# Transformer block on one core: the start-up steps of the attention stage in another order, and the gates computed by GpSimd from copies that ScalarE makes

## Reference

```python
mod = (silu(c) @ wmod).reshape(2, 6, 1, 512)
sa, ca, ga, sb, cb, gb = (mod[:, i] for i in range(6))
ga = (2 * (ga >= 0) - 1) * maximum(abs(ga), 0.25)
gb = (2 * (gb >= 0) - 1) * maximum(abs(gb), 0.25)
h = layernorm(x) * (1 + ca) + sa
x = x + ga * attention(h, Wq, Wk, Wv, Wo)      # rotary positions, causal softmax, grouped heads
h = layernorm(x) * (1 + cb) + sb
x = x + gb * ffn(h)                            # ternary weights, silu(gate) * up, rms norm
```

## Time and profile before

| | |
|---|---|
| median of 3 runs | 1857.39 us (1854.3 to 1860.57) |
| the profiled execution, its own time | 1858.29 us |
| its span in the trace | 1856.3 us |
| granted TensorE clock, mean | 0.987 |
| PE busy | 1747.3 us (94%) |
| DVE / ACT / POOL busy | 1259.0 / 1147.6 / 964.8 us |

### The profile page before, as it was taken

The page is one execution under the profiler, slowest core; times in us unless marked ns, Lnnn a source line. Parts: engine busy times, 40 slices in busy tenths (PEclk is TensorE's granted clock), DMA queues, the critical chain, the costliest instruction groups (busy, mean ns, idle before and its releaser), DMA issues. The chain is left out here.

```text
span 1856.3 us, 28089 instructions
## 1 busy us (share of the span) xinstructions
PE 1747.3 (94%) x9505; PEld 1394.7 (75%) x9505; DVE 1259.0 (68%) x2078; ACT 1147.6 (62%) x2315; POOL 964.8 (52%) x773
## 2 busy tenths in 40 slices
PE   6899999999999999999999999996999999999998
PEld 3577787777777777778777777774788778888886
DVE  5787887788788778788778878884333355545343
ACT  4578787777777777877777777784322354323322
POOL 1256667666667666666766666753000035444454
PEclk9999999999999999999999999998999999999999
DMA  6433444344344344344434434425655400101000
GB/s 229 121 94 103 120 102 124 100 109 121 88 131 114 86 123 112 92 117 108 121 103 108 125 83 134 119 82 163 208 179 177 134 29 1 52 1 51 1 29 23
DMA packets 174969, 190.95 MB, mean 103 GB/s; under 512 B 31456, under 2 KB 117736, under 8 KB 174832
## 3 DMA queue, kind: packets, MB, share of 16 engines
q1 hardware_dynamic: 137840, 140.99, 26.7%
q10 hardware_dynamic: 36992, 48.25, 9.4%
HBM read 86.12 MB, written 31.74 MB: 63 GB/s over the span
## 5 line engine op out<-in xcount | busy, mean ns | idle before, releaser
L926 DVE TENSOR_TENSOR p_lo<-ps_b,p_hi 128x512 fp32r<-128x512 f32 x576 | 395.3, 686 | 194.7 <-ACT p_hi L829 190.8
L844 ACT ACTIVATE p<-ps_b,negm 128x640 f32<-128x640 f32 (+7 forms) x512 | 381.9, 749 | 111.4 <-DVE negm L934 108.5
L829 ACT CAST p_hi<-ps_b 128x512 fp32r<-128x512 f32 x576 | 337.0, 588 | 156.9 <-PE ps_b L748 154.2
L934 DVE TENSOR_REDUCE negm<-ps_b 128x1 f32<-128x640 f32 (+7 forms) x512 | 375.8, 744 | 34.1 <-PE ps_b L738 33.4
L748 PE MATMUL ps_b<-ident,p 128*128 128x128 f32 x2304 | 350.3, 275 | 3.1 <-DVE p_lo L926 2.1
L736 PE MATMUL ps_b<-k_hh,q_hl 128*128 128x512 f32 (+3 forms) x768 | 270.1, 352 | 37.0 <-ACT p L844 36.0
L762 PE MATMUL ps_b<-p_hi,v_hl 128*128 128x512 f32 x576 | 276.9, 481 | 16.4 <-ACT o_sb L837 16.1
L748 PEld LDWEIGHTS ps_b<-ident,p 128*128 128x128 f32 x2304 | 259.0, 141 | 37.3 <-DVE p_lo L926 5.1
L737 PE MATMUL ps_b<-k_l,q_hl 128*128 128x512 f32 (+3 forms) x768 | 256.1, 346 | 0.0
L763 PE MATMUL ps_b<-p_lo,v_hl 128*128 128x512 f32 x576 | 227.6, 395 | 0.0
L736 PEld LDWEIGHTS ps_b<-k_hh,q_hl 128*128 128x128 f32 x768 | 145.1, 189 | 87.4 <-ACT p L844 54.7
(11 more groups left out here) (156 smaller groups left out, 3202.6 us busy)
## 6 DMA issues: line engine op xcount, KB each, us to landing
rot_x<-rot_s SPq DMA_DIRECT2D x320, 64.0 KB, 2.0
q_hl<-rot_s SPq DMA_DIRECT2D x128, 128.0 KB, 2.5
q_hl<-rot_x SPq DMA_DIRECT2D x128, 128.0 KB, 2.5
rd_all<-reciprocals SPq DMA_DIRECT2D x128, 128.0 KB, 3.0
o_low<-o_sb ACTq DMA_DIRECT2D x128, 128.0 KB, 2.4
attention_out<-o_sb SPq DMA_DIRECT2D x128, 128.0 KB, 2.5
o_raw<-attention_out SPq DMA_DIRECT2D x32, 512.0 KB, 4.9
wf<-in_L_ffn_w_gate_up ACTq DMA_DIRECT2D x32, 256.0 KB, 3.0
```

What stands on the lines that cost most here:

```text
L829: act.copy(p_hi[:, T % P_RING, :], ps[:, T_BANK + T % 2, :]).then_inc(phi_ready, 1)
L844: act.activation(p_32[:, parity, h, column * P:column * P + nk], s, ACT.Exp, bias=negm[:, k:k + 1], scale=1.0, accum_out=den[:, parity, k: ...
L926: dve.tensor_tensor(p_lo[:, T % P_RING, :], ps[:, T_BANK + T % 2, :], p_hi[:, T % P_RING, :].bitcast(F32), ALU.subtract).then_inc(plo_read ...
L934: dve.tensor_reduce(negm[:, k:k + 1], s, AX.X, ALU.max, negate=True).then_inc(max_ready, 1)
```

## The change

The order of the start-up changes, and who makes the gates:
- Products 0 and 1 go to PSUM banks 2 and 3; product 0 no longer waits for ScalarE's reading of n = 1. Products 1, 2 and 3 are cut into halves of two pieces; gates' products are at T = 49/53 and 58/59 and no longer between the rows of scores. The turn of late shift and scale (`LATE_TURN`) goes from T = 70 to 62.
- The gates' part of `wmod` is loaded in the prologue, before the last 512 rows of x; for this the prologue's normalised rows go to `late.h32` and `late.xn`.
- ScalarE copies the gates out of PSUM at T = 61 (two copies of 2 x 512). GpSimd makes them in five operations of 2 x 1024, all at T = 66, ahead of what it has else in that step; VectorE has no part in it. The one fused VectorE operation at the end becomes two on GpSimd. The store goes from T = 71 to 70.
- Normalising of n = 2 goes from T = 44 to 41, its statistics from 36 to 37; writing of `h` for n = 3 from T = 59 to 62 to T = 56 to 59; `hT_lo` of n = 1 in part behind the first rotary, that of n = 2 in part ahead of the rotary of qx1.
- In the start-up, ScalarE's cast, GpSimd's low part and SP's place of qy0 and qy1 come twelve steps after the use's first instead of eight, eight and ten: T = 66 and 71.
- ScalarE runs a small exponential at T = 53 (`TABLE_AT`), and the casts of the constants go from T = 52 to 60.

```diff
-        xt, xn = [x_rows[:, n] for n in range(2)], [vectors.rows_at(n) for n in range(2)]
+        xt, xn = [x_rows[:, n] for n in range(2)], [late.h32, late.xn]
@@ prologue, sync
                 sp.dma_start(vectors.late[0][:, :, v, :], wm_v[:, :, place, :]).then_inc(vectors.late_in, 16)
+            vectors.load_gates(sp, wmod)
             load_x(3, late.xt[:, 1])
@@ step numbers
-LATE_AT, LATE_TURN, LATE_ROWS = (35, 41, 64, 66), 70, (45, 45)
-GATE_LOAD, GATE_STEPS, GATE_STORE = 50, 67, 71
-ROWS_STAT, ROWS_ROOT, ROWS_NORM, ROWS_TURN = (36, 49), (41, 50), (44, 54), (48, 58)
-ROWS_MOD = ((28, 29, 30, 31), (49, 50, 51, 51), (59, 60, 61, 62))
-ROWS_LOW = ((31, 32, 33, 34), (55, 55, 56, 56), (59, 60, 61, 62))
-CONSTS_AT, KEYS_AT, QUERY_SWAP = 52, 12, 59
+LATE_AT = ((35, 0, (0, 1, 2, 3)), (41, 1, (0, 1)), (43, 1, (2, 3)), (49, 2, (0, 1)), (53, 2, (2, 3)), (58, 3, (0, 1)), (59, 3, (2, 3)))
+LATE_BANK, LATE_ROWS, LATE_TURN = (2, 3, T_BANK, T_BANK + 1), (45, 45), 62
+GATE_STEPS, GATE_STORE = (61, 66, 66, 66, 66, 66), 70
+ROWS_STAT, ROWS_ROOT, ROWS_NORM, ROWS_TURN = (37, 49), (38, 50), (41, 54), (48, 58)
+ROWS_MOD = ((28, 29, 30, 31), (49, 50, 51, 51), (56, 57, 58, 59))
+ROWS_LOW = ((31, 32, 36, 36), (50, 51, 55, 55), (59, 60, 61, 62))
+CONSTS_AT, KEYS_AT, QUERIES_AT, QUERY_SWAP, TABLE_AT = 60, 12, 12, 59, 53
@@ tensor
-                    pe.wait_ge(late.h_ready, 2 * CT)
-                vectors.product(pe, ps[0:B, T_BANK + v % 2, :], vectors.late[v // 2], v % 2).then_inc(vectors.late_done, 1)
+                i = vectors.product(pe, ps[0:B, LATE_BANK[v], :], vectors.late[v // 2], v % 2, pieces)
+                if CT - 1 in pieces:
+                    i.then_inc(vectors.late_done, 1)
@@ scalar
+                if body.before(T, GATE_STEPS[0]):
+                    act.wait_ge(vectors.late_done, 4)
+                    for v in range(2):
+                        act.copy(o_sb[0:B, v, :], ps[0:B, LATE_BANK[2 + v], :]).then_inc(vectors.gate_copied, 1)
+                if body.before(T, TABLE_AT):
+                    act.activation(den[:, 1, :], ident[:, 0:len(ROWS)], ACT.Exp)
-                for g, n, _ in body.uses(T, 8, kinds=("qx", "qy")):
+                for g, n, _ in body.uses(T, 8, kinds=("qx",)) + body.uses(T, QUERIES_AT if body.g < 0 else 8, kinds=("qy",)):
@@ gates, off VectorE and onto GpSimd
-                    dve.tensor_copy(graw, ps[0:B, T_BANK:T_BANK + 2, :]).then_inc(vectors.gate_copied, 1)
-                    gate_chain.step(dve.tensor_scalar(gsgn, graw, 0.0, 2.0, ALU.is_ge, ALU.mult))
-                    gate_chain.step(dve.tensor_scalar(gsgn, gsgn, -1.0, None, ALU.add))
-                    gate_chain.step(dve.tensor_tensor(graw, graw, gsgn, ALU.mult))
-                    dve.scalar_tensor_tensor(out=graw, in0=graw, scalar=0.25, in1=gsgn, op0=ALU.max,
-                                             op1=ALU.mult).then_inc(vectors.gates_done, 1)
+                    pool.wait_ge(vectors.gate_copied, 2)
+                    gate_chain.step(pool.tensor_scalar(gsgn, graw, 0.0, 2.0, ALU.is_ge, ALU.mult))
+                    gate_chain.step(pool.tensor_scalar(gsgn, gsgn, -1.0, None, ALU.add))
+                    gate_chain.step(pool.tensor_tensor(graw, graw, gsgn, ALU.mult))
+                    gate_chain.step(pool.tensor_scalar(graw, graw, 0.25, None, ALU.max))
+                    pool.tensor_tensor(graw, graw, gsgn, ALU.mult).then_inc(vectors.gates_done, 1)
@@ gpsimd
             def step(body, T):
+                for n in range(1, 6):
+                    if body.before(T, GATE_STEPS[n]):
+                        gate_step(n)
-                for g, n, _ in body.uses(T, 8, kinds=("qx", "qy")):
+                for g, n, _ in body.uses(T, 8, kinds=("qx",)) + body.uses(T, QUERIES_AT if body.g < 0 else 8, kinds=("qy",)):
@@ sync
-                    for g, n, _ in body.uses(T, 10, kinds=("qx", "qy")):
+                    for g, n, _ in body.uses(T, 10, kinds=("qx",)):
                         place(g, n)
+                for g, n, _ in body.uses(T, QUERIES_AT if body.g < 0 else 10, kinds=("qy",)):
+                    place(g, n)
-                if body.before(T, GATE_LOAD):
-                    sp.wait_ge(vectors.late_done, 2)
-                    vectors.load_gates(sp, wmod)
```

More of the change, by code:

```diff
@@ L101, in __init__ @@
         self.late = [flat[:, at:at + size].rearrange("p (k v e) -> p k v e", k=CT, v=2) for at in (0, 2 * GQ * 9 * P - size)]
-        self.flat = flat
         self.late_in, self.gate_in = sem("late_in"), sem("gate_in")
@@ L106, in __init__ @@
         self.gate_copied, self.gate_link, self.gates_done, self.gates_out = [sem(n) for n in ("gcopied", "glink", "gates", "gout")]
-    def rows_at(self, n):
-        size = 4 * E
-        return self.flat[:, (2 + n) * size:(3 + n) * size].rearrange("p (t e) -> p t e", t=4)
     def load_gates(self, sp, wmod):
@@ L114, in load_gates, with product @@
             sp.dma_start(self.late[1][:, :, v, :], mod_columns(wmod)[:, :, GATE[v], :]).then_inc(self.gate_in, 16)
-    def product(self, pe, out, wm, v):
-        for kc in range(CT):
+    def product(self, pe, out, wm, v, pieces=range(CT)):
+        for kc in pieces:
             i = pe.matmul(out, self.cs[:].rearrange("p (b k) -> p k b", b=B)[:, kc, :], wm[:, kc, v, :],
@@ L153, in place @@
         self.xn = sb("xn_l", [P, 2 * P_RING, 512])[:, 0:4, :]
-        self.h32 = [sb("h32_l%d" % n, [P, 2, 512]) for n in range(2)]
+        self.h32 = sb("h32_l", [P, CT, 512])
     def statistics(self, dve, n, xt):
@@ L587, in late_h32 @@
         def late_h32(n, k):
-            return spare[:, k // 2, k % 2, :] if n == 1 else late.h32[k // 2][:, k % 2, :]
+            return spare[:, k // 2, k % 2, :] if n == 1 else late.h32[:, k, :]
         @block.sync
@@ L742, in turn @@
                 if g == 0 and T == 0:
-                    pe.wait_ge(vectors.gate_copied, 1)
+                    pe.wait_ge(vectors.gate_copied, 2)
                 if j == 0:
@@ L769, in late_turns, with late_product @@
                         pe.wait_ge(late.h_ready, 2 * CT + (k + 1 if n == 3 else 0))
+                    if k == 0 and n == 2:
+                        pe.wait_ge(vectors.late_rows, 2)
                     late.turn(pe, n, k, ps[:, turned_bank(n, k), :], late.xn, ident)
-            def late_product(v):
+            def late_product(v, pieces):
                 if v == 0:
                     pe.wait_ge(vectors.late_in, 32)
-                    pe.wait_ge(late.h_ready, 2 * CT)
-                if v >= 2:
+                if v == 2 and 0 in pieces:
                     pe.wait_ge(vectors.gate_in, 32)
-                    pe.wait_ge(vectors.late_rows, v - 1)
-                vectors.product(pe, ps[0:B, T_BANK + v % 2, :], vectors.late[v // 2], v % 2).then_inc(vectors.late_done, 1)
+                i = vectors.product(pe, ps[0:B, LATE_BANK[v], :], vectors.late[v // 2], v % 2, pieces)
+                if CT - 1 in pieces:
+                    i.then_inc(vectors.late_done, 1)
             def step(body, T):
@@ L784, in step @@
                         late_turns(n)
-                for v in range(4):
-                    if body.before(T, LATE_AT[v]):
-                        late_product(v)
+                for at, v, pieces in LATE_AT:
+                    if body.before(T, at):
+                        late_product(v, pieces)
                 if body.before(T, LATE_TURN):
@@ L869, in step @@
                         act.wait_ge(vectors.late_done, v + 1)
-                        act.copy(rd_all[0:B, v, :], ps[0:B, T_BANK + v, :]).then_inc(vectors.late_rows, 1)
+                        act.copy(rd_all[0:B, v, :], ps[0:B, LATE_BANK[v], :]).then_inc(vectors.late_rows, 1)
                 if body.before(T, LATE_TURN + 1):
@@ L986, in step @@
                             late_low(n, k)
-                for n in range(5):
-                    if body.before(T, GATE_STEPS + n):
-                        gate_step(n)
                 for g, n, _ in body.uses(T, 4, kinds=("kv", "qx", "qy")):
```

16 lines of the change are left out of this document (7 added, 9 removed).

## The result

The changed kernel takes 1863.87 us (median of 15 runs, 1860.2 to 1869.15), the kernel before 1857.75 us (15 runs, 1853.35 to 1861.64). The ratio is 1.0031, 95% interval 1.002 to 1.0041: about 6 us slower, a small loss that the measurement does tell from no change. The forecast was 1857.8 with a range up to 1863.0.

A forecast was written before the change was run, and what follows sets the result against it. TensorE is busy nearly throughout from step 0, so only the start-up could change. kv10's rotary at 79.6 + 9.2 = 88.8 against 88.94 (-0.1), head start -0.5, clock +1.0: +0.4, median 1857.8 us, range 1850.0 to 1863.0.

The forecast's parts named there:

- r56: First score row of the start-up, forecast to start at 67.2 us when qx1 is placed, 3.3 us earlier.
- step 0 free: TensorE reaching step 0 of the first group at 79.3 us instead of 88.58 if nothing else is late: -9.3 us.
- The chain: Start-up followed from product 0 to step 0 with the old durations, forecast to gain 9.3 us before GpSimd's delay.
- The sum of qy0: Start-up, swap of qy0 issued by SP from 65.3, its sum forecast 4.0 us later, at 69.3.
- 79.6 + G: Forecast start of VectorE's rotary of kv10, waiting for qy0's place behind GpSimd's gates; 88.94 before.
- G: Time of GpSimd's five gate operations at T = 66: forecast 9.2 us, low end 7.9, high end 12.2.
- head start: TensorE has already done first transposes and rows of steps 0 and 1 when kv10's rotary starts: -0.5 us.
- GpSimd is far slower at compares and clamps: Rival, slower, chance 0.15: `tensor_scalar` from 3.3 us each costs over 5.6 us; at 5 us each, 1868.
- The gain is kept: Rival, faster, chance 0.19: short gate operations or a later chain leave the start-up's gain; fully kept, 1848.5 us.
- A small loss from the clock or from DMA: Rival, same, chance 0.06: qx0 at half clock or product 0 waiting for weights, +1.6 to +3, 1860 us.
- second table load: Rival without a stated chance: the load could come again for the Identity behind it, 1.3 to 2.6 us.
- Costed at nothing: Start-up parts given no cost: early gate weights, late shift and scale weights, ScalarE's gate copies, gate store.

The follow-up runs named there:

- e4: Changed kernel with GpSimd's five gate operations on 512 columns instead of 1024, gate b stored raw: 1857.38 us, ratio 1.0004 to the kernel before.
- e1: Changed kernel with the gate arithmetic back on VectorE, in four operations at T = 63, 63, 66 and 70: 1850.31 us against 1857.18 before, ratio 0.9962.
- e3: Changed kernel without the five gate operations, gates stored as raw products: 1848.42 us, ratio 0.9954 to the kernel before.
- e8: Changed kernel with 50 extra matmuls on TensorE in the hole, ahead of kv11's projection: 1863.33 us against 1861.82 before, ratio 1.0021.
- e6: Changed kernel with the same five GpSimd gate operations spread over its gaps, store in step 6: 1852.7 us against 1861.82 before, ratio 0.9956.
- e9: Kernel of e6 without the small exponential at T = 53: 1849.4 us against 1857.53 for the kernel before the change, ratio 0.9955.
- e7: Kernel of e1 without the small exponential at T = 53: 1850.33 us against 1861.82 for the kernel before the change, ratio 0.9941.
- e10: Kernel of e7 with cast, low part and place of qy0 and qy1 at the old steps: 1856.19 us against 1857.53 before the change, ratio 0.9993.

## Why the prediction was wrong

**Right: where the time goes, and by what chain.** Forecast and measured, in us: kv01 at 33.65 (34.88), qx0 at 42.6 (42.70), transposes n = 3 at 57.3 (57.61), r56 at 67.2 (67.43), end of the sum of qy1 73.8 (74.5), step 0 free at 79.3 (79.11). The chain was right in its order and its waits, but two of its sizes were off and cancelled, which was luck. kv01 came 1.2 late, since kv00's projection, at 26.84, fell into a stretch of half clock. The normalising of n = 2 behind it took 2.9 us and not the 3.9 that I had counted, so qx0 was in time all the same:

```profile
40.13 1.91 DVE L170 TENSOR_SCALAR xn_l<-xt_l,mv,rstd 128x512 f32<-128x512 f32 x4
```

The row that I had counted with has 2.88 us for the same four operations. One of the four took 1.51 us there, from 58.06, beside a low part of GpSimd (57.72 to 59.30); the others started 0.46 apart, and here nothing ran on GpSimd meanwhile. The sum of qy0 came 1.9 late (71.17 against 69.3) and that of qy1 0.7 late (73.21 against 72.5); nothing on the path waited for the first. The rotary of kv10 was to start at 79.6 + G; with the measured G of 14.2 that is 93.8, and it started at 94.09. e4 confirms the slope; for G = 0 the sum gives 79.6, and e1 and e3 have 80.64 and 80.69, 1 us later. That the hole costs a bit more than its length, by the clock, was forecast as +1.0, less a head start of 0.5. Measured: 1.15 for the clock (e8), 9.70 - 9.16 = 0.5 for the head start (from kv10 to kv11, kernel before against e8), and 5.72 - 5.15 = 0.6 for both together. The sizes fit for this hole, but not as a rule: in e4, from kv10 to kv11, the clock costs 11.45 - 9.16 = 2.3 us behind a shorter hole.

**Wrong: the term G.** I took 1.4 us for each of the three `tensor_scalar` operations, between 0.95 (a write alone) and 2.4 (a product of two inputs). They took 3.64, 2.77 and 2.76. The two products were right (2.35 and 2.33 against 2.4), so the error of G, 14.2 - 9.2 = 5.0, is all in these three. The step that failed is the upper bound: that an operation with one input can't be slower than one with two. It made 12.2 us the high end of G, where 14.2 were measured. Here one input is slower, and a second arithmetic operation in the same instruction costs more again. With the measured G, my own sum gives 79.6 + 14.2 - 88.94 + 0.5 = +5.4 us, that is 1862.8 as median, against 1863.87. The mechanism, gates in GpSimd's queue ahead of qy0's low part, was right; the term was mis-sized.

The Trainium skill, "GPSIMD Engine Reference", section 4.1, calls one-input operations on GpSimd roughly line-rate. The runs differ: 2.77 us for one input over 1024 elements where two inputs took 2.35. The measurement decides, and the estimate of 7.5 us for G by that page was further off than mine. That elementwise work belongs on VectorE holds: 0.68 against 3.64 us.

**The rivals.** "GpSimd is far slower at compares and clamps" named the mechanism, and I had given it 0.15. It was to decide from 3.3 us for each of the three (by my own sum the 5.6 us are reached at G = 14.4, so at 3.1 each); they took 3.06 on average and the loss is 6 us, so the outcome lies at that rival's near edge and not at its far end (5 us each). "The gain is kept" is what e1, e6 and e9 show when nothing that others wait for stands behind the gates: 8.8 to 8.9 us at the later place, where the chain had 9.3. "A small loss from the clock or from DMA" did not come: qx0 ran at full clock, and product 0 started right behind kv00's projection. No second table load came either: between the early one, at 53.55, and the first exponential of the scores, at 69.97, ScalarE has none. "Costed at nothing" held for the early load of the gate weights and for ScalarE's gate copies, since e1, which keeps both, has kv10's rotary within 1.1 us of its forecast place. For the early table load it held in another way than I had written: it is worth nothing in this order (e7), and in the kernel before it was not on the path, though I had named its 1.28 us among the gains.

**What the order is worth.** With the gates out of the way the new order gains 7 to 9 us by the ratios of e1 and e3, 8.8 to 8.9 by the later place. Of that, all but 1 to 2 us needs the later steps of qy0 and qy1 (e10). The later steps are also what puts qy0's low part behind the gates.

**Open.** How long TensorE's work behind a hole stays at half clock was different in each run (3 us in the changed kernel, 6 in e4), and only the changed kernel has a run that takes the clock's part out (e8). Why the sum of qy0 was 1.9 late was not looked into. Which version is the best of e1, e6, e7 and e9 is not settled either; all beat both kernels.

## What to carry to other kernels

When work is moved to an engine because that engine is idle, look at what stands behind it in the queue and who waits for that: here 14 us of work that nobody needed soon stood ahead of 1.3 us that VectorE, ScalarE and TensorE all waited for. The same work cost nothing that could be measured in gaps behind the urgent operations (e6 against e3). And where a price has no row in the trace, do not close the range with a bound from a neighbouring kind of operation: one input, two inputs and two arithmetic operations are three kinds.

## What the runs showed of the hardware

- GpSimd, float32, 2 partitions of 512 and of 1024 elements: `tensor_scalar` with compare and multiply 1.93 and 3.64 us, with one operation 1.49 and 2.77, `tensor_tensor` 1.28 and 2.35.
- The table load before an exponential does not wait for the exponential's input: 66.75 to 68.03 in e7, with the exponential at 70.48. It waits for what is ahead of it on ScalarE: in e10 it starts at 74.01, behind a cast that waited for its input until 73.23 and the short row that follows it.
- TensorE idles in the hole from 81.9; its granted clock is 1.00 until 85, 0.62 from 85 to 86, then 0.50, on into the first work behind the hole (matmuls of 0.63 us until about 98.6, later 0.40). With 50 matmuls in the hole it was 1.00 throughout.
- From kv10's rotary to kv11's it is 9.16 us with no half clock (e1, e3, e6, e8), 10.27 in the changed kernel and 11.45 in e4, so the clock behind a hole cost 1.1 and 2.3 us.
- Where a two-input operation on VectorE and one on GpSimd overlapped, the one that started later took longer, in both cases looked at. VectorE's 2 x 1024 product took 1.20 us when it started first (e1: 71.59, GpSimd's sum at 71.80, which took 2.16 instead of 1.28), and 2.33 when it started second (e7: 71.50, GpSimd's at 71.47, which took 1.28).
